# A linear-attention layer with an FP4 feed-forward block: chunks taken singly, or most of them in pairs

## The reference, cut to what matters

```python
q, k = rope(x @ Wq), rope(x @ Wk); v = x @ Wv; g = x @ Wg
scores = einsum(q / 4, k, decay)           # causal, decay[h, q, k] = gamma_h ** (q - k)
o = scores @ v
o = o * rsqrt(mean(o * o, -1) + 1e-5) * g_norm_w          # per head
x = layernorm(x + (o * silu(g)) @ Wo)
xq = fp4(x)                                # scale = max|block| / 6, round to the FP4 grid
h = silu(xq @ fp4(w_gate).T) * (xq @ fp4(w_up).T)         # 352 wide
x = layernorm(x + fp4(h) @ fp4(w_down).T)
```

## Time and profile before

| | |
|---|---|
| median of 3 runs | 140.3 us (139.18 to 141.06) |
| the profiled execution | 140.22 us, of which the span of its instructions is 137.5 us |
| PE busy | 121.0 us (88%) |
| DVE busy | 115.8 us (84%) |
| POOL busy | 102.9 us (75%) |
| ACT busy | 97.3 us (71%) |
| granted TensorE clock | 0.999 of full speed |

### The profile page before, as it was taken

How to read it: one execution, slowest core, us unless ns; L and a number is a source line. 1 busy time by engine, 2 the same in 40 slices (tenths; PEclk the granted TensorE clock), 3 DMA queues, 4 the chain that set the end, 5 groups by cost and what they waited for, 6 DMA issues and landing times.

```text
span 137.5 us, 3532 instructions
## 1 busy us (share of the span) xinstructions
PE 121.0 (88%) x1224; PEld 77.9 (57%) x1224; DVE 115.8 (84%) x438; ACT 97.3 (71%) x279; POOL 102.9 (75%) x139
## 2 busy tenths in 40 slices
PE   4986897998999999999999999999999878778650
PEld 4833354465656657585858585857575654445440
DVE  1269876867789999999999999999999899999940
ACT  3063965769787887988888888888888666665562
POOL 4204869577797979988888888889899985955692
PEclk9999999999999999999999999999999999999999
DMA  3899980000000000000000000000000000000113
GB/s 112 253 255 232 415 262 7 2 5 2 0 5 0 0 7 0 0 7 0 0 0 5 0 2 5 0 2 5 0 0 24 0 19 19 19 21 19 38 51 104
DMA packets 6897, 6.53 MB, mean 47 GB/s; under 512 B 864, under 2 KB 6112, under 8 KB 6752
## 3 DMA queue, kind: packets, MB, share of 16 engines
q1 hardware_dynamic: 5856, 5.56, 13.5%
q10 hardware_dynamic: 1024, 0.76, 1.7%
HBM read 5.26 MB, written 1.05 MB: 46 GB/s over the span
## 4 chain that ended last, share of the span: by engine, by line
PE 65%; ACT 12%; DVE 8%; DMA 5%; POOL 4%; issue 3%; SPq 1%; POOLq 0%; DVEq 0%; ACTq 0%
PE ps L464 7%; PE ps L480 7%; PE ps L352 6%; PE ps L392 5%; PE ps L335 4%; PE ps L382 4%; PE ps L326 4%; PE ps L457 3%; PE ps L471 3%; PE ps L416 3%; ACT q_eo L511 3%; PE ps L417 3%; DMA wd_nat<-in_w_down 3%; PE ps L365 3%; PE ps L449 3%
## 5 line engine op out<-in xcount | busy, mean ns | idle before, releaser
L899 POOL TENSOR_TENSOR rstd_h<-ms,minus_half 128x8 f32<-128x8 f32 x16 | 26.3, 1644 | 7.9 <-DVE ms L753 7.3
L910 POOL TENSOR_TENSOR rstd<-veps,minus_half 128x1 f32<-128x1 f32 x32 | 18.2, 571 | 1.4 <-DVE veps L769 1.2
L894 POOL TENSOR_SCALAR_AFFINE_SELECT probs<-raw 128x768 f32<-128x768 f32 x16 | 13.8, 863 | 6.9 <-ACT raw L510 6.4
L890 POOL TENSOR_TENSOR qk<-rope_c,rope_s 128x256 f32<-128x256 f32 x16 | 12.2, 766 | 8.2 <-DVE rope_s L730 7.8
L923 POOL TENSOR_TENSOR hq<-h_grid,hs 128x352 f32<-128x352 f32 x16 | 15.0, 935 | 2.9 <-DVE h_grid L667 2.9
L335 PE MATMUL ps<-w_vg,xT_sb 128*128 128x512 f32 x32 | 16.9, 610 | 0.1
L480 PE MATMUL ps<-wd_T,hT 128*128 128x128 f32 x96 | 13.6, 278 | 2.7 <-ACT hT L510 2.7
L464 PE MATMUL ps<-wgu_T,xqT 128*128 128x352 f32 x32 | 13.7, 510 | 1.1 <-DVE r L784 1.1
L480 PEld LDWEIGHTS ps<-wd_T,hT 128*128 128x128 f32 x96 | 12.1, 193 | 3.5 <-DVE r L784 2.6
L510 ACT ACTIVATE raw<-ps 128x768 f32<-128x768 f32 x16 | 13.0, 811 | 0.8 <-PE ps L352 0.6
L510 ACT ACTIVATE hT<-ps 128x384 f32<-128x384 f32 x16 | 7.8, 491 | 7.6 <-PE ps L471 7.6
(11 more groups left out here) (108 smaller groups left out, 353.6 us busy)
## 6 DMA issues: line engine op xcount, KB each, us to landing
tabs_sb<-rope_tables SPq DMA_DIRECT2D x1, 1024.0 KB, 11.2
out<-x SPq DMA_DIRECT2D x16, 64.0 KB, 1.5
tabs_sb<-rope_tables SPq DMA_DIRECT2D x1, 640.0 KB, 7.8
xT_sb<-x_transposed SPq DMA_DIRECT2D x1, 512.0 KB, 9.1
x_res<-x SPq DMA_DIRECT2D x1, 512.0 KB, 11.8
xT_sb<-x_transposed SPq DMA_DIRECT2D x1, 320.0 KB, 6.6
x_res<-x SPq DMA_DIRECT2D x1, 320.0 KB, 8.3
w_vg<-in_w_vg ACTq DMA_DIRECT2D x1, 256.0 KB, 3.4
```

The source lines that it names most:

```text
L899: gp.tensor_tensor(rstd_h[:, c, :], ms[:, c, :], minus_half[:], ALU.pow).then_inc(rms_p, 1)
L910: gp.tensor_tensor(rstd[n][:, c, :], veps[n][:, c, :], minus_half[:, 0:1], ALU.pow).then_inc(ln_p[n], 1)
```

## The change

A group of chunks takes the place of the chunk in most stages. There are ten groups, of 1, 2, 2, 2, 2, 2, 2, 1, 1 and 1 chunks. `run(stage, ahead)` now calls a stage once for group s + ahead, with one instruction over both its chunks; `run_first` and `run_second` call it for the first and for the second chunk. Stages that remain per chunk: `project_vg`, `from_state`, `next_state`, `gate`, `up`, `silu_of_gate`, `h_product`, `transpose_h`, `copy_hT`, `copy_v_and_silu`, the statistics of both norms, `ln1_centre`, `ln1_norm` and `ln2_norm`. The number of matmuls is the same. MB goes from 1 to 2: DVE masks four heads and POOL the other four. Buffers of the attention part are two deep instead of three, the PSUM banks are dealt out anew, the first layer norm's sum, the second's and the result share one buffer r, and the input loads are of 1, 2, 4 and 9 chunks. All four orders are written anew; there are 24 steps instead of 33, and ten output DMAs instead of sixteen.

```diff
-MB = 1
+MB = 2
+SIZES = [1, 2, 2, 2, 2, 2, 2, 1, 1, 1]
...
-        D = 3
-        rope_c = sb("rope_c", 128, D, 256)
+        rope_c = even_odd("rope_c", 512)
...
+        QK, QKT, VG, STATE, O, YT, ATT, XQT, GATE, UP, HT, DOWN = 4, 0, 5, 7, 2, 4, 4, 6, 6, 7, 6, 7
...
-        FIRST, LAST = -4, 29
+        FIRST, LAST = -35, -11
...
+            def run_second(stage, ahead):
+                if 0 <= s + ahead < NG and size(s + ahead) == 2:
+                    stage(first(s + ahead) + 1)
...
             for s in range(FIRST, LAST):          # PE, the new order
+                run(transpose_o, 32)
+                run_first(gate, 29)
+                run_first(up, 29)
+                run(transpose_qk, 33)
+                run(project_qk, 34)
+                run_second(gate, 29)
+                run_second(project_vg, 33)
+                if s == -30:
                     transpose_down_weights()
+                run_second(up, 29)
+                run(scores, 33)
+                run_first(transpose_h, 27)
+                run_first(project_vg, 34)
+                run(state_product, 33)
+                run_first(from_state, 33)
+                run_second(transpose_h, 27)
+                run_second(from_state, 33)
...
+                run(transpose_y, 32)
+                run(down, 26)
+                run(values, 33)
+                run(transpose_xq, 30)
+                run(out_projection, 32)
...
             for s in range(FIRST, LAST):          # DVE, the start and the end of the new order
+                run_first(h_product, 29)
+                run(rotate, 34)
+                run(h_plus_, 28)
+                run(x_plus_, 30)
+                run_first(ln1_aggr, 31)
+                run_second(h_product, 29)
+                run(mask_scores, 33)
...
+                run(mean_square, 33)
+                run(gated, 33)
+                run(x_ratio_, 31)
...
-                gp.affine_select(out=probs[:, c % 2, 2 * MB:, :], in_=raw[:, c % 2, :, :], compare_op=ALU.is_ge, fill=0.0,
-                                 base=0, pattern=[[0, NH - 2 * MB], [1, C]], channel_multiplier=-1).then_inc(mask_p, 1)
+                gp.affine_select(out=probs[:, MB:, 0:n, :, :].rearrange("p j i e q -> p j (i e) q"),
+                                 in_=raw[:, :, 0:n * 256].rearrange("p j (k q) -> p j k q", q=C),
+                                 compare_op=ALU.is_ge, fill=0.0, base=0, pattern=[[0, NP - MB], [0, 2 * n], [1, C]],
+                                 channel_multiplier=-1).then_inc(mask_p, 1)
...
             for s in range(FIRST, LAST):          # POOL, the new order
+                run(h_value, 25)
+                run(ln2_rstd, 21)
+                run(rms_rstd, 30)
+                run(gated_output, 30)
+                run(mask_scores, 31)
+                run(x_value, 28)
+                run(ln1_rstd, 29)
+                run(rotate_add, 32)
```

More of the change, by code:

```diff
@@ L20 @@
 HB = I // BLK
-MB = 1
+MB = 2
 EPS = 1e-5
+SIZES = [1, 2, 2, 2, 2, 2, 2, 1, 1, 1]
+NG = len(SIZES)
+FIRSTS = [sum(SIZES[:g]) for g in range(NG)]
 WR = I
@@ new lines, in seq_postln_kernel @@
+        hs = [sb(f"hs{m}", 128, NC * HB) for m in range(2)]
+        h_ratio = even_odd("h_ratio", 2 * I)
+        h_magic = even_odd("h_magic", 2 * I, dt=bf16)
+        h_plus = even_odd("h_plus", 2 * I)
+        h_grid = even_odd("h_grid", 2 * I)
+        hq = even_odd("hq", 2, IP)
+        hT = even_odd("hT", 2, 3, C)
+        wr_ratio, wr_magic, wr_plus = ([buf[:, 0, 0:WG], buf[:, 1, 0:I]] for buf in (h_ratio, h_magic, h_plus))
+        ps = ctx.enter_context(nc.psum_tensor("ps", [128, 8, 512], f32))
@@ L320, in warm_up, with project_qk @@
                     mm(ps[:, 7, 0:C], ident[:], ident[:], start=True, stop=True)
-            def project_qk(c):
+            def project_qk(g):
                 pe.wait_ge(d_wqk, 16)
[L324 to L328, removed]
+                pe.wait_ge(d_x[load_of(first(g))], 16)
+                free(QK)
+                for i in range(size(g)):
+                    last = mm(ps[:, QK, i * 256:(i + 1) * 256], xT(first(g) + i), w_qk[:], start=True, stop=True)
+                last.then_inc(qk_pe, 1)
+                fill(QK, "qk")
+                if g == 0:
                     warm_up(4)
@@ L347, in scores, with transpose_qk @@
-            def scores(c):
-                pe.wait_ge(qkT_act, 3 * (c + 1))
+                pe.wait_ge(d_x[load_of(c)], 16)
+                free(VG)
+                mm(ps[:, VG, :], xT(c), w_vg[:], start=True, stop=True).then_inc(vg_pe, 1)
+                fill(VG, "vg")
+            def transpose_qk(g):
+                pe.wait_ge(c_ident, 1)
+                if tile.get(QKT) != "qk" or filled["qk"] > g + 1:
+                    free(QKT)
+                pe.wait_ge(qk_p, g + 1)
+                n = size(g)
+                for m in range(2):
+                    for i in range(n):
+                        k = (m * n + i) * C
+                        last = transpose(ps[:, QKT, k:k + C], qk[:, g % 2, i, m * 128:(m + 1) * 128], ident[:])
+                last.then_inc(qkT_pe, 1)
+                fill(QKT, "qkT")
@@ L412, in out_projection, with transpose_o @@
-            def out_projection(c):
-                pe.wait_ge(c_wo, 1)
-                free_vg_bank()
-                pe.wait_ge(yT_act, c + 1)
-                mm(att_ps, yT[:, c % 2, 0, :], wo_s[:, 0, :], start=True, stop=False)
-                mm(att_ps, yT[:, c % 2, 1, :], wo_s[:, 1, :], start=False, stop=True).then_inc(att_pe, 1)
-                fill(5, "att")
+            def transpose_o(g):
+                if tile.get(O) != "sc" or filled["sc"] > g + 1:
+                    free(O)
+                pe.wait_ge(oT_act, g + 1)
+                for k in range(2 * size(g)):
+                    last = transpose(ps[:, O, k * C:(k + 1) * C], oT[:, g % 2, k, :], ident[:])
+                last.then_inc(tr_pe, 1)
+                fill(O, "o")
@@ new lines, in transpose_y, with out_projection @@
+            def transpose_y(g):
+                if tile.get(YT) != "sc" or filled["sc"] > g + 1:
+                    free(YT)
+                pe.wait_ge(y_p, g + 1)
+                for k in range(2 * size(g)):
+                    last = transpose(ps[:, YT, k * C:(k + 1) * C], y[:, g % 2, k * C:(k + 1) * C], ident[:])
+                last.then_inc(yT_pe, 1)
+                fill(YT, "yT")
+            def out_projection(g):
+                pe.wait_ge(c_wo, 1)
+                if tile.get(ATT) != "yT" or filled["yT"] > g + 1:
+                    free(ATT)
+                pe.wait_ge(yT_act, g + 1)
+                for i in range(size(g)):
+                    for m in range(2):
+                        last = mm(ps[:, ATT, i * H:(i + 1) * H], yT[:, g % 2, 2 * i + m, :], wo_s[:, m, :], start=m == 0,
+                                  stop=m == 1)
+                last.then_inc(att_pe, 1)
+                fill(ATT, "att")
@@ L481, in down @@
                 last.then_inc(down_pe, 1)
[L482 removed]
+                fill(DOWN, "down")
             warm_up(4)
             for s in range(FIRST, LAST):
[L486 to L494 removed]
@@ L495, in _ @@
[L495 to L505 removed]
+                run, run_first, run_second = stage_runner(s)
+                run(transpose_o, 32)
+                run_first(gate, 29)
```

808 lines of the change are left out of this document (401 added, 407 removed).

## The result

The changed kernel takes 141.94 us (141.8 to 143.91, 4 runs), the kernel before 140.49 beside it: ratio 1.018, 95% interval 1.012 to 1.025. It is 1.8% slower where 3.7% faster was forecast. All ratios are taken over fast runs alone (those within 1.5% of the fastest of their kernel), so they are not the quotients of the medians. The profiled execution has a span of 139.8 us against 137.5. Busy time fell on ACT (97.3 to 87.3 us) and POOL (102.9 to 91.1) as the merging promised; on DVE it rose, 115.8 to 116.3, where the prediction had it fall by about 4.

What follows compares the result with a forecast made beforehand. Three limits in turn: the loop through four engines, PE with DVE close behind, then DVE. +3.4 - 10.1 + 2.2 - 0.7 = -5.2 us from 140.22 gives 135.0 us; own range 132 to 137.5, wide range 130 to 142.

Steps and rivals of the forecast that it cites:

- the price of a VectorE instruction: DVE throughout: 1.03 ns an element plus 0.07 us fixed; six pairs and four single chunks take 4.4 us less.
- I take nothing: DVE instructions over 4-dimensional views in pairs: no extra cost assumed; upper bound 4 us in all.
- POOL is held up by longer DVE instructions: Rival, chance 0.16: POOL's elementwise work in loop and full steps delayed, 10.3 us together, giving 145.3 us.
- I cost both at nothing: PE's waits in project_qk for ln1_sum and in from_state for the mask: no cost; a late mask 0 to 1 us.
- Start to chunk 1: Span start to transpose_o of chunk 1: 21.6 us instead of 18.2, so 3.4 us late.
- The loop: Early chain through four engines, values round to values: 9.4 us for a pair instead of 11.9 for two chunks.
- Pair steps 3 to 7: Ten chunks in five steps, bounded by loop, PE or DVE: 52.1 us against 62.2, gain 10.1.
- The gain is given back: Rival, chance 0.24: DVE idles more before step 8, 0.7 us in each of six pair steps, giving 139.2 us.
- Steps 8 to 10: Single attention, paired feed-forward work, to the last chunk's transpose_o: 28.9 us against 26.7, 2.2 given back.
- The drain to the last gate: DVE's backlog after the last transpose_o, 7.0, 5.0 and 4.0 us, to the last gate at 118.6 us.
- The tail: Serial end after the last gate, with queued powers and norms: 13.7 us against 13.45 before.
- DVE's busy total lower by about 4 us: Sign expected in the new trace, from merged DVE instructions over the whole kernel.

Runs made afterwards that it cites:

- eps_per_chunk: Changed kernel with ln_eps as one instruction of one element per chunk instead of one of two elements for a pair: ratio 0.9956 to the kernel before.
- before_eps2: Kernel before the change with ln_eps over two elements instead of one, same number of instructions: ratio 1.0177 to the unedited kernel before.
- bank7_wait: Changed kernel; the first state_product after the weights' transposes waits only for the gate and up weights' copy, as bank 7 needs: ratio 1.0064 to the kernel before.
- before: The kernel before the change, with single chunks: 140.49 us beside the changed kernel.
- eps_and_bank7: Also called "both edits": changed kernel with the edits of eps_per_chunk and bank7_wait together: 138.05 us, ratio 0.9894 to the kernel before.
- after: The changed kernel without further edits: 141.94 us, ratio 1.018 to the kernel before.
- before_mb2: Kernel before the change with MB = 2 alone, its orders and single chunks as they are: ratio 0.9942 to the unedited kernel before.

## Why the prediction was wrong

The direction was wrong. The measured time of 141.94 us lies just inside the wide range (130 to 142), but that range was meant for a gain that is partly given back, and the forecast itself was 132 to 137.5.

Two terms of the sum failed. The first is the price of a VectorE instruction: "That is 1.03 ns an element and 0.07 fixed. A pair saves only the fixed part of 20 instructions". It prices each instruction as if GpSimd didn't run beside it, and counts every merge as 0.07 us saved. For the big ones the price was right wherever nothing held them: h_ratio took 0.88 us where about 0.85 was foreseen. (The doubt about 4-dimensional views, at which "I take nothing" stands, isn't the fault either: the pair's addition has a plain row of two numbers.) The cost came in the smallest, ln_eps: with two elements instead of one it stood still until GpSimd's running instruction ended, up to 1.2 us. eps_per_chunk (3.2 us by the ratios, 2.3 at like clocks) and before_eps2 (2.5 us) show it from both sides, with a strided and with a contiguous pair of numbers.

The rival that named the mechanism had it the wrong way round: "POOL is held up by longer DVE instructions". Both directions occur (the earlier trace rows showed one). Its own sign didn't come: POOL's product of a pair took 1.09 us on average, not 1.8. POOL's h_value of a pair was held, by about 0.6 us in five of six (1.96 to 2.04 against 1.38), but POOL had idle time, and VectorE, from step 8 on, had none. What POOL's delays cost by themselves was not tested. The rule of the port lock, in the Trainium skill, "SBUF — State Buffer", section "SBUF: two separate sides", says that of the two engines' instructions that need the shared ports the one that starts second blocks, either way. The traces here agree for GpSimd's products, rotate additions and masks (the ends at 114.34 and 114.37 us). Where an addition began only 0.04 us after a rotate_add, it was held twice and not held four times in before_eps2. The traces don't agree for GpSimd's powers: VectorE's x_ratio, on two SBUF operands, ran from 45.16 in 0.41 us, its usual time, inside a power that ran from 44.72 to 47.63, and an addition of two elements that began at 132.86, after a power's start at 132.77, took 0.15. The Trainium skill, "VectorE: DVE Perf Modes", section "Mode 2×_2P — use both read ports for one tensor", says that a tensor_scalar on SBUF operands, fp32 too, can read one tensor through both ports. What the traces show is that an addition of two elements waits and one of one element doesn't (408 and 335 ns against 134 and 143); that this mode is the reason is inferred from the page.

The second is "I cost both at nothing", of the bank waits. The two that were walked through did little (the steps came within 0.6 us of the forecast), though one of the named signs did appear: the weight loads of from_state wait 0.37 us for next_state once in each pair step. The wait that cost was a third, in the code of `free` for the weights, in step 4 alone: 1.7 us by the ratios of bank7_wait, 1.4 at like clocks.

Point by point:

- Start to chunk 1: 21.6 predicted, 21.41. The first mean_square came at 14.69 us, 15.8 predicted. The power for a pair: 2.87 predicted, 2.91. The loop: 9.4 predicted, 9.93.
- Pair steps 3 to 7: 52.1 predicted, 54.2 measured, 52.9 once the wait on bank 7 is gone. The gain over before, the prediction's largest term, is there: 62.2 to 54.2.
- The rival "The gain is given back" comes nearest in time. Its mechanism, more idle time of VectorE before step 8, isn't what happened: 10.7 us in steps 2 to 7 where 11.5 were counted, and 9.0 with both edits.
- Steps 8 to 10: 28.9 predicted, 30.4. An excess of 0.53 us stands in h_ratio each time, 1.6 in all. That removing it would shorten the steps isn't shown: with another POOL order half of it fell on x_grid and x_plus, and the steps were 0.3 us shorter.
- The drain to the last gate: 16.0 predicted, 19.35, of which 1.2 go with both edits (18.13). Of the 2.1 left, 1.2 are VectorE's (busy 17.24 us where its sum was put at 16.0) and 0.9 are idle time, which taking VectorE's sum leaves out; the power above, 0.7 us longer than elsewhere, lies in this stretch.
- The tail: 13.7 predicted, 14.4, and 13.8 with both edits.
- "DVE's busy total lower by about 4 us": it rose by 0.5. (By its own prices, 0.87 less for each of six pairs and 0.27 more for each of four single chunks, the sum is 4.2, not 4.4.) With both edits it is 114.0, 1.8 lower. What is missing is of the size of the stand-stills that remain in that run: 1.6 us in h_ratio, 1.1 in the weights' instruction beside the rotate_add at 19.1 us.

The span was 7.4 us longer than predicted (139.8 to 132.4). The two faults account for 3.4 of it by the two profiled spans (139.8 to 136.4). The other 4.0 lie before the last transpose_o (1.9) and in the drain (2.1), as the table shows. Held instructions of both engines stand in both places, but no experiment took them out without putting others in, so the cause of these 4.0 stays open. The forecast of the sign would have been right without the two faults: eps_and_bank7 is 1.1% faster than before, still not the 3.7% forecast.

## What to carry to other kernels

When instructions are merged, look at the smallest ones too: here a VectorE tensor_scalar in SBUF that grew from one element per partition to two began to wait for GpSimd, and a merge that saves 0.06 us cost up to 1.1 each time. A waiting instruction of that kind counts as busy; compare the mean, the minimum and the maximum of each shape, not the busy share. And a stall that comes only once, early, on the engine that bounds is paid in full: read each wait of a new buffer rule for the case that happens once. When two kernels differ by 1 or 2%, compare runs at the same granted clock.

## What the runs showed of the hardware that was not expected

- VectorE's 128x2 tensor_scalar ended within 0.04 us of GpSimd's instruction in all 18 long cases (5 in after, 13 in before_eps2); at 128x1 no such wait is seen in the 32 instances of before (135 to 154 ns).
- GpSimd's powers did not hold VectorE (0.41 us for x_ratio inside a power of 2.91 us). One power stood still itself when h_grid began 0.03 us after it (1.26 us instead of 0.55).
- VectorE at 99.5% busy did not bound the kernel (before_mb2), and at 99% it carried most of the chain that ended last (steps 8 to 10 of after, 30.14 of 30.39 us). The share doesn't tell the two apart.
